# Sixteen-head attention, two layers in one launch: how the row maximum is subtracted before a softmax

## The reference

```python
x = x + L0_attn(layernorm(x))   # qkv with bias, 16 heads of 8, logits/sqrt(8) - softplus(alpha_h)*|i-j|, softmax, out proj
x = x + L0_ffn(layernorm(x))    # tanh(h @ W @ A1 @ A2 + bias)
x = x + L1_attn(layernorm(x))   # latent kv, scores/sqrt(128) * exp(-0.01*|i-j|), softmax, out proj
x = x + L1_ffn(layernorm(x))    # 256 -> 512 -> 512 -> 128 with weights +1/-1 from booleans, relu
```

## Time and profile before

| | |
|---|---|
| time, median of 3 | 350.02 us (349.3 to 350.71) |
| profiled execution, span from first to last instruction | 348.83 us; the page gives no other time for it |
| mean granted TensorE clock | 0.985 of full |
| TensorE busy | 330.2 us (95%) |
| DVE busy | 275.9 us (79%) |
| ScalarE busy | 271.7 us (78%) |
| GpSimd busy | 261.3 us (75%) |
| the chain that ended last | TensorE 74%, DVE 9%, DMA 5%, issue 4%, ScalarE 3%, GpSimd 2% |

### The profile page before, as it was taken

The page is one execution under the profiler, slowest core; times in us unless marked ns, Lnnn a source line. Parts: engine busy times, 40 slices in busy tenths (PEclk is TensorE's granted clock), DMA queues, the critical chain, the costliest instruction groups (busy, mean ns, idle before and its releaser), DMA issues.

```text
span 348.8 us, 11196 instructions
## 1 busy us (share of the span) xinstructions
PE 330.2 (95%) x3550; PEld 244.0 (70%) x3550; DVE 275.9 (79%) x1367; ACT 271.7 (78%) x586; POOL 261.3 (75%) x655
## 2 busy tenths in 40 slices
PE   6599979999999999999999999999999999999986
PEld 4276757777776777777666767777787777778675
DVE  6877778898988998989988888768777677668246
ACT  3576874877776777777878889989898898888943
POOL 7368665676767666767969899898998988898430
PEclk9969998999999999999999999999999999999999
DMA  5202532223233323232332223224132331111001
GB/s 141 69 1 70 161 118 77 97 78 111 84 105 92 95 85 103 78 110 83 105 96 93 80 88 105 74 76 127 36 108 63 89 115 41 43 34 48 2 17 30
DMA packets 42390, 28.14 MB, mean 81 GB/s; under 512 B 9111, under 2 KB 38494, under 8 KB 42334
## 3 DMA queue, kind: packets, MB, share of 16 engines
q1 hardware_dynamic: 41768, 27.18, 26.4%
q10 hardware_dynamic: 566, 0.26, 0.3%
HBM read 14.09 MB, written 13.09 MB: 78 GB/s over the span
## 4 chain that ended last, share of the span: by engine, by line
PE 74%; DVE 9%; DMA 5%; issue 4%; ACT 3%; POOL 2%; SPq 1%; POOLq 0%; DVEq 0%; ACTq 0%
PE bank L551 20%; PE bank L566 14%; PE bank L548 8%; PE bank L592 7%; PE bank L526 5%; PE bank L540 5%; PE bank L613 4%; PE bank L605 3%; DVE scored L854 3%; DMA den_rows<-dden 3%; PE bank L574 2%; PE bank L658 1%; DMA dacc<-acc_sb 1%; PE bank L758 1%; POOL scored L1332 1%
## 5 line engine op out<-in xcount | busy, mean ns | idle before, releaser
L1093 ACT ACTIVATE probs<-bank 128x512 f32<-128x512 f32 x256 | 147.9, 599 | 47.6 <-PE bank L551 31.7
L854 DVE CUSTOM_DVE_ANT_0 scored<-bank,decay 128x256 f32<-128x256 f32 x256 | 93.1, 417 | 28.4 <-PE bank L526 28.2
L551 PE MATMUL bank<-ident,scored 128*128 128x128 f32 x736 | 108.6, 279 | 2.2 <-ACT probs L1093 1.4
L1332 POOL TENSOR_SCALAR scored<-scored,negbias 128x256 f32<-128x256 f32 x224 | 105.5, 487 | 3.1
L854 DVE CUSTOM_DVE_ANT_0 scored<-bank,adist 128x256 f32<-128x256 f32 x256 | 93.1, 417 | 11.0 <-PE bank L526 7.8
L551 PEld LDWEIGHTS bank<-ident,scored 128*128 128x128 f32 x736 | 81.8, 142 | 27.1 <-issue 19.4
L566 PE MATMUL bank<-probs,vpad 128*32 128x256 f32 x1024 | 69.2, 388 | 0.0
L1323 POOL TENSOR_SCALAR negbias<-mx 128x2 f32<-128x2 f32 x144 | 32.8, 237 | 32.0 <-DVE mx L854 31.1
L548 PE MATMUL bank<-ident,scored 128*128 128x128 f32 x288 | 44.4, 278 | 0.0
L566 PEld LDWEIGHTS bank<-probs,vpad 128*32 128x32 f32 x1024 | 26.9, 109 | 24.9 <-ACT probs L1093 7.2
L854 DVE DVE_READ_ACCUMULATOR2_ANT mx<- 128x1 f32 x512 | 42.1, 82 | 0.0
(11 more groups left out here) (196 smaller groups left out, 442.7 us busy)
## 6 DMA issues: line engine op xcount, KB each, us to landing
dqk<-parts SPq DMA_DIRECT2D x120, 64.0 KB, 2.0
stack<-dqk SPq DMA_DIRECT2D x30, 256.0 KB, 2.8
dacc<-acc_sb SPq DMA_DIRECT2D x15, 256.0 KB, 2.2
att_rows<-dacc SPq DMA_DIRECT2D x15, 128.0 KB, 2.6
den_rows<-dden SPq DMA_DIRECT2D x15, 128.0 KB, 2.5
out_dram<-outb SPq DMA_DIRECT2D x7, 128.0 KB, 1.8
x_sb<-in_L_attn_x_dram SPq DMA_DIRECT2D x1, 640.0 KB, 4.7
den_in<-acc_sb SPq DMA_DIRECT2D x30, 8.0 KB
```

Of the source, the lines that this page charges most:

```text
L551: mm = pe.transpose(dst, src, ident[:, :])
L854: red = dve.tensor_tensor_reduce(scored[:, r, t, :], bank[c % QUAD][:, t * T:(t + 1) * T], tab[:, (1 - t) * P:(1 - t) * P + T], 1.0, NEG_B ...
L1093: act.activation(probs[:, c % RING, :, :], turn_bank(c)[:, :].rearrange("p (a c) -> p a c", a=2), ACT.Exp).then_inc(probs_ready, 1)
L1332: sh = pool.tensor_scalar(scored[:, r, t, :], scored[:, r, t, :], negbias[:, 2 * r + t:2 * r + t + 1], 1.0, ALU.add, ALU.mult)
```

## The change

P heads are no longer used: SHIFT now has G 10, D 3, A 3 in layer 0 and G 7, D 6, A 3 in layer 1. The A and G forms no longer wait for a negated maximum: they compute mx - score straight from mx (multiply by -1, then add mx), and the exp of such a head takes the scale -1. The tile negbias goes. SHIFT_LAG, SLOTS, FIRST and two bank choices (SHARED) are set anew. The boolean tables and the scalars are issued by SP in items 1 to 3, behind sp_bounce, instead of in item 0. The bound of the exp's wait on pv_done is written another way, with the same value.

```diff
-SHARED = ({"qk": 1, "v": 7, "ft": 7, "f0": 7, "proj": 7, "xn": 1},
-          {"qk": 1, "v": 7, ...
+SHARED = ({"qk": 1, "v": 7, "ft": 7, "f0": 7, "proj": 7, "xn": 2},
+          {"qk": 1, "v": 0, ...
 SLOTS = {
-    "qk": (6, 2), "v": (2, 1), "xn": (14, 15), "att": (15, 14), "proj": (15, 14), "ft": (7, 3), "f0": (10, 13),
-    "h0": (8, 9), "h1": (15, 11), "h2a": (15, 15), "h2b": (0, 0), "h3a": (1, 5), "h3b": (4, 7), "out": (0, 11),
-    "qk_out": (6, 2), "v_out": (4, 1), "xn_out": (14, 14), "acc_out": (4, 4), "norm": (12, 10), "f_norm": (4, 0),
-    "ft_out": (7, 3), "f0_out": (11, 9), "h0_out": (13, 9), "h1_out": (15, 12), "h2_out": (1, 0), "h3_out": (12, 7),
-    "stats0": (6, 4), "stats1": (7, 4), "mean": (7, 8), "hi": (12, 6), "rden": (9, 10), "proj_out": (16, 15),
-    "f_stats0": (0, 0), "f_stats1": (2, 0), "f_mean": (2, 0), "out_out": (7, 12),
-    "low": (11, 7), "pool_norm": (10, 8), "bias": (12, 5), "pool_ffn": (1, 0), "f0_add": (14, 0), "low_in": (1, 5),
-    "low0": (7, 10), "low1": (15, 13), "low2": (0, 3), "low3": (6, 8),
+    "qk": (6, 2), "v": (2, 1), "xn": (14, 15), "att": (15, 14), "proj": (15, 14), "ft": (9, 3), "f0": (11, 6),
+    "h0": (0, 9), "h1": (15, 11), "h2a": (7, 15), "h2b": (4, 0), "h3a": (1, 6), "h3b": (4, 7), "out": (0, 10),
+    "qk_out": (6, 2), "v_out": (5, 1), "xn_out": (14, 14), "acc_out": (4, 4), "norm": (10, 10), "f_norm": (4, 0),
+    "ft_out": (9, 4), "f0_out": (12, 6), "h0_out": (15, 9), "h1_out": (13, 12), "h2_out": (0, 0),
+    "h3_out": (13, 7), "stats0": (6, 0), "stats1": (8, 4), "mean": (8, 5), "hi": (11, 7), "rden": (9, 8),
+    "proj_out": (16, 15), "f_stats0": (0, 0), "f_stats1": (0, 0), "f_mean": (1, 0), "out_out": (6, 12),
+    "low": (13, 7), "pool_norm": (9, 6), "bias": (12, 7), "pool_ffn": (1, 0), "f0_add": (15, 11),
+    "low_in": (3, 8), "low0": (10, 9), "low1": (13, 13), "low2": (1, 7), "low3": (5, 8),
 }
...
-SHIFT = ("PPGP" "DGGD" "GDPP" "PPGA", "GGGD" "GGAP" "PGDG" "AGAG")
+SHIFT = ("GGDG" "DGAG" "GADG" "GGAG", "DGDG" "ADDG" "DGDG" "AGAG")
...
-SHIFT_LAG = ("3322212123212121", "1211122323112212")
+SHIFT_LAG = ("1121332133213312", "2123132232212111")
...
         if c % 4 == 0:
-            need(act, pv_done, c // 4 - 1)
+            need(act, pv_done, c // 4 + 1 - RING // 4)
         act.activation(probs[:, c % RING, :, :], turn_bank(c)[:, :].rearrange("p (a c) -> p a c", a=2),
-                       ACT.Exp).then_inc(probs_ready, 1)
+                       ACT.Exp, scale=-1.0 if shift_of(c) in "AG" else 1.0).then_inc(probs_ready, 1)
...
-        act.wait_ge(shift_b, shifts("AG", c + 1))
+        act.wait_ge(max_ready, c + 1)
         for t in range(QT):
             sh = act.activation(scored[:, r, t, :], scored[:, r, t, :], ACT.Identity,
-                                bias=negbias[:, 2 * r + t:2 * r + t + 1])
+                                bias=mx[:, 2 * r + t:2 * r + t + 1], scale=-1.0)
...
-        out, done = (negmax, shift_p) if shift_of(c) == "P" else (negbias, shift_b)
-        pool.tensor_scalar(out[:, 2 * r:2 * r + 2], mx[:, 2 * r:2 * r + 2], -1.0, None, ALU.mult).then_inc(done, 1)
+        pool.tensor_scalar(negmax[:, 2 * r:2 * r + 2], mx[:, 2 * r:2 * r + 2], -1.0, None, ALU.mult).then_inc(shift_p, 1)
...
-        pool.wait_ge(shift_b, shifts("AG", c + 1))
-        for t in range(QT):
-            sh = pool.tensor_scalar(scored[:, r, t, :], scored[:, r, t, :], negbias[:, 2 * r + t:2 * r + t + 1], 1.0,
-                                    ALU.add, ALU.mult)
+        pool.wait_ge(max_ready, c + 1)
+        for t in range(QT):
+            sh = pool.tensor_scalar(scored[:, r, t, :], scored[:, r, t, :], -1.0, mx[:, 2 * r + t:2 * r + t + 1],
+                                    ALU.mult, ALU.add)
...
-            if c >= 1 and shift_of(c - 1) in "PAG":
+            if c >= 1 and shift_of(c - 1) == "P":
                 pool_shift(pool, c - 1)
...
-            if i == 0:
-                for n in range(3):
-                    sp.dma_start(s_cols[:, n:n + 1], a[f"L1_ffn_s{n}"].partition_broadcast(P)).then_inc(ld_s, 16)
-                for lo, hi, name in ((0, 2, "L1_ffn_k0"), (2, 6, "L1_ffn_k1")):
-                    sp.dma_start(bool_raw[:, lo * FEAT:hi * FEAT].rearrange("p (n f) -> p n f", f=FEAT),
-                                 a[name].rearrange("(n p) f -> p n f", p=P)).then_inc(ld_bool, 16)
-                sp.dma_start(bool_raw[:, 6 * FEAT:6 * FEAT + 4 * D].rearrange("p (n f) -> p n f", n=4),
-                             a["L1_ffn_k2"].rearrange("(n p) f -> p n f", p=P)).then_inc(ld_bool, 16)
...
             if has(i + 2):
                 sp_bounce(sp, i + 2)
+            if i == 1:
+                for n in range(3):
+                    sp.dma_start(s_cols[:, n:n + 1], a[f"L1_ffn_s{n}"].partition_broadcast(P)).then_inc(ld_s, 16)
+            for k, (lo, hi, name) in enumerate(((0, 2, "L1_ffn_k0"), (2, 6, "L1_ffn_k1"))):
+                if i == 1 + k:
+                    sp.dma_start(bool_raw[:, lo * FEAT:hi * FEAT].rearrange("p (n f) -> p n f", f=FEAT),
+                                 a[name].rearrange("(n p) f -> p n f", p=P)).then_inc(ld_bool, 16)
+            if i == 3:
+                sp.dma_start(bool_raw[:, 6 * FEAT:6 * FEAT + 4 * D].rearrange("p (n f) -> p n f", n=4),
+                             a["L1_ffn_k2"].rearrange("(n p) f -> p n f", p=P)).then_inc(ld_bool, 16)
```

More of the change, by code:

```diff
@@ L57 @@
 LAG = 4
+SCORE_AT = 1
 PV_LAG = 9
@@ L61 @@
 MISC = 7
-SHARED = ({"qk": 1, "v": 7, "ft": 7, "f0": 7, "proj": 7, "xn": 1},
-          {"qk": 1, "v": 7, "ft": 7, "f0": 7, "h3": 7, "h0": 0, "h1": 7,
-           "out": 1, "proj": 1, "xn": 0, "h2": 7})
+SHARED = ({"qk": 1, "v": 7, "ft": 7, "f0": 7, "proj": 7, "xn": 2},
+          {"qk": 1, "v": 0, "ft": 7, "f0": 7, "h3": 7, "h0": 0, "h1": 7, "out": 1, "proj": 1, "xn": 0, "h2": 7})
 STARTING = {0: {'xn': 2, 'v': 0}, 1: {'xn': 2, 'qk': 7}}
@@ L82 @@
 SLOTS = {
-    "qk": (6, 2), "v": (2, 1), "xn": (14, 15), "att": (15, 14), "proj": (15, 14), "ft": (7, 3), "f0": (10, 13),
-    "h0": (8, 9), "h1": (15, 11), "h2a": (15, 15), "h2b": (0, 0), "h3a": (1, 5), "h3b": (4, 7), "out": (0, 11),
-    "qk_out": (6, 2), "v_out": (4, 1), "xn_out": (14, 14), "acc_out": (4, 4), "norm": (12, 10), "f_norm": (4, 0),
[3 rows of a table removed]
-    "low": (11, 7), "pool_norm": (10, 8), "bias": (12, 5), "pool_ffn": (1, 0), "f0_add": (14, 0), "low_in": (1, 5),
-    "low0": (7, 10), "low1": (15, 13), "low2": (0, 3), "low3": (6, 8),
+    "qk": (6, 2), "v": (2, 1), "xn": (14, 15), "att": (15, 14), "proj": (15, 14), "ft": (9, 3), "f0": (11, 6),
[6 more added lines that the diff above has]
+    "low_in": (3, 8), "low0": (10, 9), "low1": (13, 13), "low2": (1, 7), "low3": (5, 8),
 }
 FIRST = {
[3 rows of a table removed]
-    "w2_out": 14, "wkv": 0, "brow": 4,
[3 rows of a table added]
+    "w2_out": 15, "wkv": 0, "brow": 4,
 }
 ORDER = [HALF * r + 2 * j + e for r in range(2) for e in range(2) for j in range(4)]
-SHIFT = ("PPGP" "DGGD" "GDPP" "PPGA", "GGGD" "GGAP" "PGDG" "AGAG")
+SHIFT = ("GGDG" "DGAG" "GADG" "GGAG", "DGDG" "ADDG" "DGDG" "AGAG")
 def shift_of(c):
@@ L247, in program @@
     negmax = sb("negmax", [P, 2 * RING], F16)
-    negbias = sb("negbias", [P, 2 * RING])
     ident16 = sb("ident16", [P, P], F16)
@@ L382, in program @@
     shift_d = sem("shift_d")
-    shift_b = sem("shift_b")
     shift_a = sem("shift_a")
@@ L673, in pe_iteration @@
             c = H * i + s
-            if s % QUAD == 1:
+            if s % QUAD == SCORE_AT:
                 pe_scores(pe, i, s // QUAD)
@@ L1557, in _ @@
             pool_iteration(pool, i)
-        if shift_of(HEADS - 1) in "PAG":
+        if shift_of(HEADS - 1) == "P":
             pool_shift(pool, HEADS - 1)
```

## The result

The changed kernel takes 358.34 us (median of 4 runs, 357.89 to 358.91) against 350.17 for the kernel before on the same chip: a ratio of 1.0254, interval 1.0207 to 1.0301. The forecast was 336.5. The profiled execution took 357.89 us, its span 356.1, at a granted clock of 0.986.

The account below looks back on a forecast made before the run. TensorE was taken to set the pace from item 2 on, with DVE becoming at least an equal bound in layer 0. Terms summed to -13.2 us, 336.8 from 350.02, stated as 336.5; forecast 333.5 to 340.5, range 331.5 to 342.

Parts of the forecast that it names:

- DVE: a D head costs 0.61: Layer 1: price in us of a D head on DVE; four more per item take DVE from 15.88 to 18.3.
- 18.3 of DVE and 15.0 of GpSimd fit into 20.9: Layer 1, items 10 to 15: TensorE stays the bound at 20.9 us per item, saving 6 x 0.46 = 2.8 us.
- the att_t multiply: Layer 0: might wait one GpSimd instruction, 0.47 us, once per item, 3.3 us over seven items; left out of the sum.
- Items 2 and 3: 15.8 + 0.3 = 16.1: Layer 0: 15.8 us of work plus 0.3 of uncovered wait per item, 1.25 us saved each.
- Items 4 to 7: 16.3 + 0.3 = 16.6: Layer 0: DVE's 16.3 us plus 0.3 of wait per item, from 70.65 to about 67.0 with 0.6 of stalls.
- Rival B: Layer 0 gains almost nothing because the denominators' copies pace it and it keeps 17.0 us; 342.4 us in all, chance 0.14.
- Items 8 and 9 at -0.4: Both items together: relief of GpSimd helps, four more D heads hurt; each 0.5 us slower to 2 faster.
- Item 1 at -2.8: 1.5 us from P heads less 0.4, 0.8 of den_in wait, even odds on the clock's 1.7; bounds -1 and -4.5.
- den_in can come sooner: Item 1: with the table loads moved away, den_in issues 0 to 2.1 us earlier; 0.9 taken, halving the DVE wait.
- The turned sign costs nothing: A and G heads: new sign form taken as zero cost; scores come some 0.3 us sooner, no gain where TensorE is full.
- Rival C: Slower: TensorE waits once per group and its clock falls in items 1 to 9, up to 360 us; chance 0.05.
- Loads on SP hidden: Moved load issues on the sync queue fall where it waits for the bounce anyway; exposed 0.5 us, counted as hidden.

Follow-up runs that it names:

- the kernel with the other form: Changed kernel, but DVE's subtract of D heads also writes the row maximum of its result to an unread accumulator tile; 352.5 us, ratio 1.0112 to the kernel before.

## Why the prediction was wrong

- *"DVE: a D head costs 0.61"*, and from it *"18.3 of DVE and 15.0 of GpSimd fit into 20.9"*. This is the step that failed and turned the sign: items 10 to the end were to gain 3.0 us and lost 7.2, half of the 20.5 us between forecast and result. The price was read where GpSimd worked on 128x2 only, and used where GpSimd runs long instructions; the mean of a subtract became 502 ns. The sums of both engines were each right to about 1 us without the exclusion (18.77 and 15.86 in the kernel with the other form), and can't be put side by side while they exclude each other. Shown: the change of form gives 5.8 us back. The rest, 1.4, is not all explained; part of it is the wait for att_t. The rule was even at hand: the prediction used it for the att_t multiply alone, rated it at 3.3 us and didn't ask which other DVE instruction it names. (For att_t itself the fear didn't come true: 15 of them take 7.6 us in all, 8.5 before.) GpSimd's 15.0 was too low because a negation was priced at 0.23: the twelve that the sign form removes from item 12 gave back 2.1 us (20.11 to 18.03), 0.17 each.
- *"Items 2 and 3: 15.8 + 0.3 = 16.1"*, *"Items 4 to 7: 16.3 + 0.3 = 16.6"*: measured 17.11 and 17.73, then 17.2, 18.1, 17.0 and 17.2, so 1.2 to 2.3 us over TensorE's 15.81, and -6.1 became -1.0. TensorE's floor of 15.81 is an estimate that no run reached (the spacing of the matmuls is as in the earlier trace rows), but DVE as *"at least an equal bound"* was wrong: halving its maxima leaves 17.04. What lay just under TensorE's 17.34 wasn't an engine's total; the chains point to two loops through several engines, 17.0 and 17.5 us long, and the cause stays open as far as an experiment goes. Rival B had this place right (*"layer 0 keeps 17.0"*) and, if the second loop counts, half of its mechanism: den_in's turn in the queue, not the six slots after the reciprocal.
- *Items 8 and 9 at -0.4*: +1.2. DVE is busy 18.80 of item 8's 18.83 us, where 18.2 were forecast as "as long as the item already is": DVE is the bound there, and what it gained in work (four D heads) is what the item lost. The other form doesn't help, since it is itself longer (37.5 us for the two, DVE busy 18.86 of 18.89); with the old kinds item 8 is back at 17.79. The term had the right place and the wrong sign.
- *Item 1 at -2.8*: -3.5, but item 0 +2.8 for -0.9. Between the profiles of before and of the later loads alone the pair differs by 1.8, nearly all of it the clock that doesn't fall, for which the prediction had even odds; the loads as its cause are not shown; *"den_in can come sooner"* by 0.9 didn't happen (0.1). Item 0 takes 21.6 to 24.1 us in the profiles with the tables of before and 24.9 to 26.6 in those with the new ones, so the tables lengthen it, by 2.8 us in the mean; item 0 and 1 together 40.9 to 43.7 and 42.7 to 45.6. Each is one execution in which the granted clock of item 0 differs (0.75 to 1.00), and which of the moved steps does it isn't settled.
- *The turned sign costs nothing*: the duration holds within the 10% allowed (501 ns for 487), but *"brings A and G scores some 0.3 us sooner: no gain where TensorE is full"* missed that it moves GpSimd's subtract onto DVE's: items of layer 0 are 0.22 longer with it, those of layer 1 0.24 shorter.
- *Rival C*: the clock is 1.00 in the windows of all items from 1 on, although TensorE stands for 1.47 us at 257.61. It was slower, but not by the clock; C's sign came true by another cause.
- *Loads on SP hidden*: right. They stand in the loop above, but in the next round SP waits as long (2.4 us) for the bounce's own data.

## What to carry to other kernels

Before work is moved from one engine to another, read from the trace beside what the price was measured, not only the price: here DVE's subtract in SBUF and GpSimd's long instructions could not run side by side, and a form with an accumulator at 476 ns was cheaper than one of 340 that waits for up to 0.9 us. Look at the spread of a line's durations too. A bound engine can hide chains that are just below it: when an engine is relieved by 1.5 us, look for the chain that is 0.3 us shorter, which no engine's busy time shows. And where a part of a change is a new order of everything (SLOTS), time the rest without it first.

## What the runs showed of the hardware

- A DVE subtract of 128x256 fp32 in SBUF that begins while a GpSimd subtract or product has over 0.2 us left ends 0.145 to 0.154 us after that one (70 cases): 0.34 us becomes 0.57 beside a subtract of 0.51, up to 1.25 beside a product of 1.16 to 1.21 us, and four in a row took 3.74. Beside GpSimd's instructions on 128x2 it isn't longer.
- The other way round, a GpSimd subtract that begins inside such a DVE subtract ends 0.341 to 0.348 us after it: 507 to 616 ns for 478 (31 cases), and 480 to 492 when DVE's has the form with the accumulator (71 cases).
- The DVE multiply for att_t (128x256, two inputs in SBUF) ended 0.27 to 0.29 us behind the GpSimd instruction that was running when it began: 0.42 us became 0.76 before (item 6) and 1.22 in the kernel with the other form (items 13 to 15).
- The same operation with an accumulator takes 462 to 478 ns whatever GpSimd does, plus a read of 71 to 86 ns that overlaps the next.
- Waits of TensorE of 1.44, 1.77 and 1.89 us (the kernel before, that with two A heads turned back, that with the old FIRST) were followed by half the clock for 3.4 to 3.5 us; one of 1.28 (sign form alone) at the place of the 1.44 was not, nor one of 0.41, nor one of 1.47 us in item 12 after.
